# Spectra with exchanged halves, copied by the sync queue, for one full-width cross product in a metaformer block

## The chip, the cores and the metric

The kernel runs on one core of a Trainium2 chip. The metric is the device time of one execution in microseconds (us). A difference of about 0.2% (1.05 us) is what a measurement of this kernel can tell from no change.

The core has five engines that run side by side and wait for each other by semaphores: TensorE (PE, matrix products into PSUM), VectorE (DVE), ScalarE (ACT), GpSimd (POOL) and SyncE (SP), which here only issues transfers. Sixteen DMA engines carry the transfers of all queues.

## The reference, cut to what matters

One block of a network on 16 images of 128 channels and 16x16 pixels: a convolution branch with a Fourier filter, then a mixture of 8 experts with the best two taken for each token.

```python
xp  = star_scale * square(relu(einsum('bhwc,mc->bhwm', xc, w_pw1))) + star_bias   # 256 channels
xf  = rfft2(xp, axes=(1, 2), norm='ortho')
weight         = einsum('bfc,hwf->bhwc', routeing, complex(cw))      # complex, 4 filters mixed
spatial_weight = einsum('bfc,hwf->bhwc', spatial_routeing, spatial_weights)
xs  = irfft2(xf * weight, ...)
out = einsum('bhwm,dm->bhwd', xp * spatial_weight + xs, w_pw2)
x   = x + out
t   = layernorm(tokens(x));  x = x + experts(t)                      # top 2 of 8
```

The part that matters is `xf * weight`, a complex product: `re = xr*wr - xi*wi`, `im = xi*wr + xr*wi`. The second product of each needs the imaginary part where the real part stands, and the other way round.

## The kernel before

**Tiling.** The 16 images are worked on as 8 pairs. In a first stage ("phase A", 0 to about 90 us) each pair's pixels become `star` (the `xp` of the reference) and its spectrum `spec`. For each pair i and each parity e (0 or 1) of the vertical frequency, `spec[:, e, i, :]` is a tile of 128 partitions by 512 columns: the real parts are in partitions 0 to 63 and the imaginary parts in 64 to 127 (a few real-only frequencies fill the rest). Then routing weights are worked out once (90 to 130 us), and each of them is laid out over `RS` by eight small transfers, five on the sync queue and three on GpSimd's (`routing_rows`, line 356).

**The filter stage** ("phase B", 130 to about 217 us) is a software pipeline with one step for each pair (`filter_loop`: steps 0 to 2 written out, 3 to 6 in a loop of two steps, step 7 written out). In step i:

- TensorE makes six weight tiles of pair i+1 (`filters`, L810) in three PSUM banks that are used in turn; n = 0, 1 are the spatial weights, n = 2 and 4 the real parts and n = 3 and 5 the imaginary parts for e = 0 and 1. Between them it projects pair i-1 (L844), turns pair i back to pixels (`branch`, L828 and L834), transposes normalised tokens of pair i-2 (L853) and makes their expert logits (L859).
- VectorE makes the products of pair i+1 for e = 0 (`filter_products`): `prod` = spectrum times real weight (L1095, 128 x 512), and `cross` = exchanged spectrum times imaginary weight, in two instructions of 64 partitions (L1098, L1099), which read one half of the spectrum and write the other half of `cross`. It adds the branch to the tokens of pair i-1 (`residual`, L1104) and takes their statistics (L980, L984), makes the products for e = 1, waits for GpSimd's `rstd` and normalises the tokens of pair i-1 (L990, four instructions of 128 x 128 that write `xn`), and copies logits (L1116).
- GpSimd makes the inverse standard deviation (`inv_std`, L436 and L438), adds `prod` and `cross` of pair i+1 (`spectral`, L499, two instructions) and multiplies `star` with the spatial weights of pair i+2 (`spatial`, L493, two instructions), in this order once a step has its rhythm.
- ScalarE copies between PSUM and SBUF (L620, L625, L630).
- The sync queue stores each pair's normalised tokens (`store_tn`, L399). After the store of pair 5 it issues the loads of the experts' weights `w1` and `w3` (L407, L408), which lie where `star` lay.

**Afterwards** (217 to 257 us) the weights are split into high and low parts and the tokens are sorted by expert; then 71 tiles of tokens run through the experts (257 to 500 us), with indirect gathers and scatters by GpSimd; a last stage adds up the results (to 525 us).

What the steps below touch: `filter_products` and its callers in VectorE's program, `store_tn` and the lines around it in SyncE's, `inv_std`, `spectral` and `spatial` in GpSimd's, `filters` in TensorE's, and the tile `rw2`, a weight that is read for the last time by the matrix products of L785, before `r_mm` is signalled.

## Time and profile before

| what | us |
|---|---|
| median of three runs | 527.25 |
| the three runs | 526.24, 527.25, 527.28 |
| the profiled execution | 526.45 |
| its span in the profile | 524.7 |
| outside the span | 1.75 |

| engine | busy us | share of the span |
|---|---|---|
| PE | 390.1 | 74% |
| DVE | 255.3 | 49% |
| POOL | 246.8 | 47% |
| ACT | 168.1 | 32% |

The shares are means over stages with different limits. The page draws them in 40 slices of 13.1 us; in the slices of the filter stage (130 to 217 us) both PE and DVE show 8 or 9 tenths, and after it DVE falls to 2 or 3. The chain of work that ended last passes in the filter stage mainly through DVE and POOL, and from 257 us on mainly through PE. The clock of PE was granted at full speed (2.4 GHz) from 136.5 to 221.8 us and at half (1.2 GHz) in the 20 us before.

### The profile page before, as it was taken

What the parts mean: (1) busy time and instruction counts of PE and PEld (TensorE: products, weight loads), DVE (VectorE), ACT (ScalarE), POOL (GpSimd) and SP (SyncE); (2) the same over time, 40 slices, a digit from 0 to 9 for tenths busy, and PEclk for the clock granted to TensorE, in tenths of its full rate; (3) what the DMA queues carried; (4) which work ended last, traced back from release to release, by engine and by line L of the source; (5) the groups of instructions that cost most, each with busy time, mean ns of one, the idle gap of its engine ahead of it and who ended that gap; (6) DMA issues with size and microseconds to landing.
All of it is one profiled execution on the core that took longest, in us unless ns stands there. A gap on an engine that the chain in (4) does not pass through costs nothing.

```text
span 524.7 us, 7887 instructions
## 1 busy us (share of the span) xinstructions
PE 390.1 (74%) x2272; PEld 319.2 (61%) x2273; DVE 255.3 (49%) x637; ACT 168.1 (32%) x387; POOL 246.8 (47%) x265
## 2 busy tenths in 40 slices
PE   0899899860999888699497877967878687886700
PEld 0565555650587767556397776867877587875700
DVE  5377664440789999729732322332323332333236
ACT  0544444020123231343043333333323333333233
POOL 7224423412774465100255655556556566664434
PEclk9999999795799999969587979797979988899855
DMA  8910000003001000730011111111111111111184
GB/s 247 223 40 2 0 0 0 6 5 35 2 0 41 20 20 21 280 141 1 15 36 41 47 33 43 35 39 41 35 40 40 40 35 45 40 44 31 36 303 178
DMA packets 14081, 29.94 MB, mean 57 GB/s; under 512 B 4392, under 2 KB 5564, under 8 KB 13548
## 3 DMA queue, kind: packets, MB, share of 16 engines
q1 hardware_dynamic: 7388, 17.93, 11.3%
q0 software_dynamic: 4784, 9.52, 6.7%
q10 hardware_dynamic: 1888, 2.23, 1.2%
q8 instruction: 11, 0.18, 0.1%
q14 instruction: 10, 0.08, 0.0%
HBM read 20.24 MB, written 8.85 MB: 55 GB/s over the span
## 4 chain that ended last, share of the span: by engine, by line
PE 50%; DVE 17%; issue 10%; DMA 6%; another core or an unknown queue 5%; ACT 5%; POOL 4%; SPq 1%; POOLq 1%; DVEq 0%; ACTq 0%
PE bank L953 14%; PE bank L935 11%; DVE xn L990 7%; PE bank L928 6%; PE bank L895 2%; DMA RS<-r_hl 2%; PE bank L783 2%; PE bank L922 2%; PE bank L726 2%; PE bank L734 2%; POOL shared L499 2%; ACT shared L676 2%; DVE st L980 1%; PE bank L914 1%
## 5 line engine op out<-in xcount | busy, mean ns | idle before, releaser
L524 POOL DMA_INDIRECT y_dram<-shared,idx_scatter x71 | 69.9, 985 | 80.0 <-DVE shared L1248 68.2
L935 PE MATMUL bank<-spec,shared 128*128 x426 | 71.6, 311 | 39.0 <-ACT shared L676 36.7
L519 POOL DMA_INDIRECT shared<-tn_dram,idx_gather x71 | 68.8, 969 | 58.8 <-DVE idx_gather L1238 37.4
L935 PEld LDWEIGHTS bank<-spec,shared 128*128 128x128 f32 x426 | 61.3, 216 | 46.1 <-issue 45.7
L1258 DVE TENSOR_TENSOR shared<-shared,bank 128x384 f32<-128x384 f32 x71 | 39.2, 552 | 70.6 <-issue 36.6
L1243 DVE TENSOR_TENSOR xgt_hl<-bank,xgt_hl 128x128 fp32r<-128x128 f32 x71 | 20.7, 291 | 90.2 <-ACT xgt_hl L671 85.1
L953 PE MATMUL bank<-RS,xgt_hl 128*128 x142 | 59.4, 419 | 0.1
L683 ACT ACTIVATE shared<-bank 128x384 f32<-128x384 f32 x71 | 34.8, 491 | 68.3 <-PE bank L953 49.1
L990 DVE TENSOR_SCALAR xn<-T,mv,rstd 128x128 f32<-128x128 f32 (+1 forms) x64 | 51.3, 872 | 3.7 <-POOL rstd L438 3.1
L953 PE MATMUL bank<-w_hi,xgt_hl 128*128 x142 | 51.8, 365 | 0.0
L671 ACT ACTIVATE xgt_hl<-bank 128x128 fp32r<-128x128 f32 x71 | 19.7, 277 | 75.7 <-PE bank L922 57.3
L928 PE MATMUL bank<-ident,shared 128*128 128x128 f32 x213 | 38.1, 291 | 6.9 <-issue 5.1
L676 ACT ACTIVATE shared<-bank 128x384 f32<-128x384 f32 x71 | 35.0, 492 | 22.5 <-PE bank L928 17.0
L953 PE MATMUL bank<-w_lo,xgt_hl 128*128 x142 | 40.0, 366 | 0.0
L810 PE MATMUL bank<-RS,coef 128*128 128x512 f32 (+1 forms) x48 | 21.4, 504 | 22.0 <-DMA RS<-r_hl 15.5
L928 PEld LDWEIGHTS bank<-ident,shared 128*128 128x128 f32 x213 | 29.0, 151 | 13.0 <-issue 8.1
L436 POOL TENSOR_SCALAR var_eps<-mv 128x4 f32<-128x4 f32 x16 | 3.7, 228 | 68.9 <-DVE mv L984 68.8
L745 PE MATMUL bank<-xp,sp 128*64 128x256 f32 x288 | 33.6, 387 | 0.0
L834 PE MATMUL bank<-inv,shared 128*128 128x256 f32 x128 | 30.4, 380 | 1.8 <-POOL shared L499 1.8
L953 PEld LDWEIGHTS bank<-RS,xgt_hl 128*128 128x128 f32 x142 | 30.6, 215 | 1.3 <-issue 1.1
L953 PEld LDWEIGHTS bank<-w_hi,xgt_hl 128*128 128x128 f32 x142 | 30.3, 213 | 0.0
L953 PEld LDWEIGHTS bank<-w_lo,xgt_hl 128*128 128x128 f32 x142 | 28.9, 210 | 0.0
(175 smaller groups left out, 685.2 us busy)
## 6 DMA issues: line engine op xcount, KB each, us to landing
star<-y_dram SPq DMA_DIRECT2D x16, 256.0 KB, 5.5
star<-in_w SPq DMA_DIRECT2D x2, 1536.0 KB, 8.4
tn_dram<-xn SPq DMA_DIRECT2D x8, 256.0 KB, 2.0
out<-T ACTq DMA_DIRECT2D x8, 256.0 KB, 2.5
spec<-in_w SPq DMA_DIRECT2D x1, 1536.0 KB, 7.1
shared<-in_sp_even SPq DMA_DIRECT2D x1, 1280.0 KB, 14.6
shared<-tn_dram,idx_gather POOLq DMA_INDIRECT x71
y_dram<-shared,idx_scatter POOLq DMA_INDIRECT x71
```

Source lines behind the costliest of these rows:

```text
L519: pool.indirect_dma_start(xg[j % BUFS], None, tn_dram, bass.IndirectOffsetOnAxis(ap=idx_gather[:, j:j + 1], axis=0)).then_inc(S[f"g_x{j % ...
L524: pool.indirect_dma_start(y_dram, bass.IndirectOffsetOnAxis(ap=idx_scatter[:, j:j + 1], axis=0), yo[j % BUFS], None).then_inc(S[f"y_out{j ...
L676: act.activation(hidt[u], p_ht[u][:, 0:HID], ACT.Copy).then_inc(S["f_hts"], 1)
L683: act.activation(silu[u], p_h1[u][:, 0:HID], ACT.Silu).then_inc(S["f_silu"], 1)
L745: mm = pe.matmul(ps_conv[u][HALF * g:HALF * g + HALF, 0:PIX], sp1[:, t, :], xp[:, u, g, t // 3:t // 3 + SIZE, t % 3:t % 3 + SIZE], start=( ...
L810: pe.matmul(ps_w[n % 3][:, :], coef[:, ring[n], :], RS[:, :, :, ds(i, 1), :].rearrange("r c g b m -> r g c (b m)"), start=True, stop=True)\
L834: mm = pe.matmul(ps_v[u][m][:, g * PIX:(g + 1) * PIX], y_c[u][e][:, g * MED + m * P:g * MED + (m + 1) * P], inv[:, e, :], start=False, sto ...
L928: mm = pe.transpose(p_ht[u][:, c * P:(c + 1) * P], hid[u][:, c * P:(c + 1) * P], ident[:, :])
L935: mm = pe.matmul(p_y[:, 0:DIM], hidt[u][:, c * P:(c + 1) * P], w2s[:, c, ds(e * DIM, DIM)], start=(c == 0), stop=(c == HC - 1))
L953: mm = pe.matmul(psum[:, 0:HID], xgt[u][xs], w_hl[ws][:, cols], start=(n == 0), stop=(n == 2))
L990: op = dve.tensor_scalar(xn[:, u, t, :], flat(T[:, ds(i * 4 + t, 1), :]), mv[:, u, t, 0:1], rstd[:, u, t:t + 1], ALU.subtract, ALU.mult)
L1258: dve.tensor_tensor(hid[u], silu[u], p_h3[u][:, 0:HID], ALU.mult).then_inc(S["f_act"], 1)
```

## The change

`filter_products` now makes `cross` in one instruction of 128 partitions, from a copy of the spectrum whose halves are exchanged. The copy of pair i, both parities, lies in one of two tiles, `rw2` (even pairs) and a new tile `turned_b` (odd pairs), 4 KiB in each partition. It is made by two transfers of the sync queue, each of 64 partitions x 2 rows x 512 floats (256 KiB), from SBUF to SBUF. The copies of pairs 0 to 3 stand in front of the first token store, that of pair i+4 behind the store of pair i; each waits until the tile's last reader (`b_cross` of pair i-2 of its own number) is through. VectorE waits for the copy by a semaphore for each of the two tiles.

```diff
+        turned_b = sb("turned_b", [P, NF * MED])
+        turned = [t[:].rearrange("p (e n) -> p e n", e=2) for t in (rw2, turned_b)]
...
+            def turn_spectrum(i, u):
+                wait_apart(sp, S["a_spec"], i * 2 + 2)
+                wait_done(sp, S["b_cross"], i * 2 - 2)
+                for lo, hi in ((0, 64), (64, 0)):
+                    sp.dma_start(turned[u][lo:lo + 64], spec[hi:hi + 64, :, ds(i, 1), :].rearrange("p e i n -> p e (i n)"))\
+                        .then_inc(S[f"b_turned{u}"], 16)
...
-            store_tn(0, 0)
-            store_tn(1, 1)
-            with sp.Fori(1, PAIRS // 2 - 1) as n:
-                for u in range(2):
-                    store_tn(n * 2 + u, u)
+            sp.wait_ge(S["r_mm"], 1)
+            for i in range(4):
+                turn_spectrum(i, i % 2)
+
+            def store_and_turn(i, u):
+                store_tn(i, u)
+                if i + 4 < PAIRS:
+                    turn_spectrum(i + 4, u)
+            for i in range(PAIRS - 2):
+                store_and_turn(i, i % 2)
...
-            def filter_products(i, e):
+            def filter_products(i, u, e):
...
                 dve.wait_ge(S["b_w"], i * 6 + n_s + 1)
-                dve.tensor_tensor(cross[e][0:64], spec_at(64, P, e, i), ps_w[n_s % 3][0:64, :], ALU.mult)
-                dve.tensor_tensor(cross[e][64:P], spec_at(0, 64, e, i), ps_w[n_s % 3][64:P, :], ALU.mult)\
+                dve.wait_ge(S[f"b_turned{u}"], (i - u) * 16 + 32)
+                dve.tensor_tensor(cross[e], turned[u][:, e, :], ps_w[n_s % 3][:, :], ALU.mult)\
                     .then_inc(S["b_cross"], 1)
```

How the rows stand on two engines. First VectorE, in the second half of the loop body of the filter stage: the products of e = 0, the residual and its statistics, the products of e = 1. Line numbers of the changed kernel are 18 higher from here on; ISA and REGISTER_ALU rows are register work. Before:

```order
L1095 TENSOR_TENSOR shared<-spec,bank2 128x512
L1097 REGISTER_ALU
L1098 ISA
L1098 TENSOR_TENSOR shared<-spec,bank0 64x512
L1099 TENSOR_TENSOR shared<-spec,bank0 64x512
L1104 ISA
L1104 TENSOR_TENSOR T<-T,bank7 128x512
```

The same place in the changed kernel:

```order
L1113 TENSOR_TENSOR shared<-spec,bank2 128x512
L1115 REGISTER_ALU
L1117 TENSOR_TENSOR shared<-turned_b,bank0 128x512
L1122 ISA
L1122 TENSOR_TENSOR T<-T,bank7 128x512
```

One instruction of 128 partitions stands where two of 64 stood, with one more semaphore in its wait; nothing else of VectorE's order moves. The products of e = 1 change in the same way.

Second SyncE, from the spreading of the routing weights to the experts' weights. Before:

```order
L356 DMA RS<-r_hl 4x32x128 x5
L399 DMA tn_dram<-xn 128x512 x2
...
L399 DMA tn_dram<-xn 128x512
L398 REGISTER_ALU
L399 ISA
L399 DMA tn_dram<-xn 128x512
...
L407 DMA star<-in_w1 128x3072
```

In the changed kernel:

```order
L360 DMA RS<-r_hl 4x32x128 x5
L405 DMA rw2<-spec 64x2x512 x2
L405 DMA turned_b<-spec 64x2x512 x2
L405 DMA rw2<-spec 64x2x512 x2
L405 DMA turned_b<-spec 64x2x512 x2
L410 DMA tn_dram<-xn 128x512
L405 DMA rw2<-spec 64x2x512 x2
L410 DMA tn_dram<-xn 128x512
...
L410 DMA tn_dram<-xn 128x512 x2
L425 DMA star<-in_w1 128x3072
```

Eight pairs of transfers are new; the last of them stands behind the store of pair 3, and between the store of pair 5 and the load of `w1` nothing is new.

## Rows read from the trace of the kernel before

**Rows 1.** Busy time by stretch: us, then PE, PEld, DVE, ACT, POOL, PEclk, DMA share, GB/s.

```profile
144.90:157.10 12.20, 11.97 (x75) 10.56 (x76) 10.40 (x19) 3.06 (x6) 8.73 (x8) 1.00 0.00 0
189.75:200.76 11.01, 9.61 (x60) 8.13 (x59) 10.62 (x20) 2.90 (x5) 6.19 (x6) 1.00 0.06 24
```

**Rows 2.** DVE in order of time, one step: start us, us, line, operation [idle before].

```profile
189.86 0.68 DVE L1095 TENSOR_TENSOR shared<-spec,bank 128x512 f32<-128x512 f32 x1
190.57 0.68 DVE L1098 TENSOR_TENSOR shared<-spec,bank 64x512 f32<-64x512 f32 x1
191.26 0.69 DVE L1099 TENSOR_TENSOR shared<-spec,bank 64x512 f32<-64x512 f32 x1
191.99 0.69 DVE L1104 TENSOR_TENSOR T<-T,bank 128x512 f32 x1
...
193.76 0.38 DVE L984 BATCH_NORM_AGGREGATE mv<-st 128x2 f32<-128x6 f32 x4
194.13 0.69 DVE L1095 TENSOR_TENSOR shared<-spec,bank 128x512 f32<-128x512 f32 x1
194.85 0.68 DVE L1098 TENSOR_TENSOR shared<-spec,bank 64x512 f32<-64x512 f32 x1
195.54 0.69 DVE L1099 TENSOR_TENSOR shared<-spec,bank 64x512 f32<-64x512 f32 x1
196.27 4.46 DVE L990 TENSOR_SCALAR xn<-T,mv,rstd 128x128 f32 x4
```

**Rows 3.** POOL in order of time, the same step.

```profile
194.29 0.23 POOL L436 TENSOR_SCALAR var_eps<-mv 128x4 f32<-128x4 f32 x1 [4.66 <-DVE mv L984]
194.68 1.04 POOL L438 TENSOR_TENSOR rstd<-var_eps,mhalf 128x4 f32<-128x4 f32 x1 [0.15 <-POOL var_eps L436]
195.69 2.49 POOL L499 TENSOR_TENSOR shared<-shared 128x512 f32<-128x512 f32 x2
198.15 2.49 POOL L493 TENSOR_TENSOR shared<-star,shared 128x512 f32<-128x512 f32 x2
```

**Rows 4.** L990 where POOL is idle (215 to 217 us): duration ns min/median/max.

```profile
L990 DVE TENSOR_SCALAR xn<-T,mv,rstd x4: 337/340/347, 215.7 to 216.5; 128x128 f32<-128x128 f32 x4
```

**Rows 5.** Phase A, DVE and POOL at 61 us: the race behind rstd.

```profile
61.20 1.56 DVE L990 TENSOR_SCALAR xn<-T,mv,rstd 128x128 f32 x2
61.35 1.33 POOL L444 TENSOR_TENSOR buf<-star 128x512 f32 x1 [0.25 <-DVE star L997]
```

**Rows 6.** The second half of cross, all 16: duration ns, first and last start us.

```profile
L1099 DVE TENSOR_TENSOR shared<-spec,bank x16: 691/692/692, 133.2 to 206.5; 64x512 f32<-64x512 f32 x16
```

**Rows 7.** PE in order of time: the transposed tokens, then the two waits of a step.

```profile
190.05 0.60 PE L853 MATMUL bank<-ident,xn 128*128 128x128 f32 x4
...
194.87 0.50 PE L810 MATMUL bank<-RS,coef 128*128 x1 [0.48 <-DVE shared L1095]
196.29 0.51 PE L810 MATMUL bank<-RS,coef 128*128 x1 [0.92 <-DVE shared L1099]
```

**Rows 8.** PE in order of time at the start of the filter stage.

```profile
130.12 3.19 PE L810 MATMUL bank<-RS,coef 128*128 128x512 f32 x6 [15.46 <-DMA RS<-r_hl]
133.11 3.54 PE L734 MATMUL bank<-buf,fwd 128*128 128x512 f32 x4
137.44 0.97 PE L810 MATMUL bank<-RS,coef 128*128 128x512 f32 x3 [0.78 <-DVE spec L1003]
```

**Rows 9.** DVE in order of time there: cross of pair 0, spectrum of pair 7.

```profile
132.50 0.68 DVE L1098 TENSOR_TENSOR shared<-spec,bank 64x512 f32<-64x512 f32 x1
...
136.05 1.33 DVE L1003 COPY spec<-bank 128x512 f32<-128x512 f32 x2
```

**Rows 10.** DVE in order of time: cross of pair 2, behind PE.

```profile
147.19 0.68 DVE L1098 TENSOR_TENSOR shared<-spec,bank 64x512 f32<-64x512 f32 x1 [1.59 <-PE bank L810]
```

**Rows 11.** Busy time by stretch: loads of 128 and 64 partitions, the wait for RS.

```profile
8.00:11.00 3.00, 0.00 (x0) 0.00 (x0) 3.00 (x6) 0.00 (x0) 3.00 (x2) 1.00 1.07 398
17.00:22.00 5.00, 5.00 (x27) 2.99 (x27) 1.82 (x4) 2.23 (x4) 0.74 (x1) 1.00 0.97 203
122.00:130.00 8.00, 0.00 (x0) 0.00 (x0) 0.00 (x0) 0.00 (x0) 0.00 (x0) 0.50 0.24 26
```

**Rows 12.** SP's queue in order of time: w1 is issued.

```profile
210.49 0.35 SPq L407 DMA_DIRECT2D star<-in_w  x1
```

**Rows 13.** ACT in order of time: the first use of w1.

```profile
217.11 2.76 ACT L648 ACTIVATE RS<-star 128x3072 fp32r<-128x3072 f32 x1 [2.89 <-DMA star<-in_w]
```

More of the change, by code:

```diff
@@ L333, in metaformer @@
             "r_log r_max r_sub r_exp r_sum r_rec r_norm r_tr r_hi r_lo r_rows r_rows_pool b_w b_sw b_p b_cross b_u b_y "
-            "b_vt b_vts b_w2 b_t b_stats b_aggr b_eps b_rstd b_norm b_tn0 b_tn1 b_tr b_tnt "
+            "b_vt b_vts b_w2 b_t b_stats b_aggr b_eps b_rstd b_norm b_turned0 b_turned1 b_tn0 b_tn1 b_tr b_tnt "
             "b_gate b_logit q_iota q_zero q_tri q_dve q_ready q_exp_done q_count q_oh_tile q_oh_ready q_oh_used "
@@ L1154, in phase_b @@
                 if not last(i, PAIRS):
-                    filter_products(i + 1, 0)
+                    filter_products(i + 1, 1 - u, 0)
                 if not first(i):
@@ L1158, in phase_b @@
                 if not last(i, PAIRS):
-                    filter_products(i + 1, 1)
+                    filter_products(i + 1, 1 - u, 1)
                 else:
@@ L1168, in phase_b @@
                     logit_copy(i - 2, u)
-            filter_products(0, 0)
-            filter_products(0, 1)
+            filter_products(0, 0, 0)
+            filter_products(0, 0, 1)
             spectrum_copy(PAIRS - 1)
```

## The prediction

> **What bounds the kernel now.** I read the page first (shares by engine, the 40 slices, the chain that ended last), then the busy time by stretch, then one step of the filter stage in order of time on DVE, POOL and PE. The page says that no engine bounds the whole; the stretches say where this change can act. In a steady step of the filter stage, 11.01 us long, DVE is busy 10.62 us, PE 9.61 and POOL 6.19 [rows 1]. But DVE's busy time is not all work. The four instructions of L990 take 4.46 us in it [rows 2], and 0.34 us each where POOL is idle [rows 4]. In the step they end one by one at the ends of POOL's four instructions of L499 and L493, which run back to back from 195.69 to 200.64 us [rows 3]: each L990 waits until the POOL instruction that was running before it has ended. So the step is a ring of two engines:
>
> DVE makes prod and cross of e = 0 and the residual (189.86 to 192.68), statistics (to 194.14) [rows 2]; POOL makes rstd (to 195.72), then L499 twice and L493 twice (to 200.64) [rows 3]; the last L990 ends with them at 200.73, and DVE begins the next step.
>
> Two things follow. The cross of e = 0 lies on this ring. The cross of e = 1 (194.85 to 196.23) does not: it lies beside POOL's rstd and the first L499, and what it gives back is waited away again in front of L990.
>
> The filter stage is followed by a chain that begins with its end: the store of pair 5's tokens, the issue of w1 at 210.49, w1's first use at 217.11 [rows 12, 13].
>
> **The change part by part.**
>
> *The cross of e = 0.* From the start of L1098 to the start of the residual are 191.99 - 190.57 = 1.42 us [rows 2]. One instruction of 128 x 512 from SBUF and PSUM, as L1095 is, takes 0.68 to 0.69 us, and with the gap behind it 0.71 (190.57 - 189.86) [rows 2]. So a step loses 1.42 - 0.71 = 0.71 us. The ring's other parts keep their lengths: behind the statistics come 0.15 us, L436, L438 and the 4.95 us of L499 and L493 as before.
>
> How many steps get it? The products of eight pairs are made, 16 second halves in all [rows 6]. For pairs 0 and 1 PE is the bound (below). For pair 2 the cross starts at 147.19, behind PE's weight tile [rows 10], and PE has no gap in the whole of that step (11.97 of 12.20 us [rows 1]); but the residual stands behind the cross on DVE and needs only PE's projection, which has ended by then, so this cross already shortens the ring. Pairs 2 to 7 make six steps: 6 x 0.71 = 4.26 us.
>
> *The cross of e = 1.* It would end at 195.54 instead of 196.23, and the norm behind it needs rstd, which ends at 195.72 [rows 2, 3]. DVE then meets POOL's first L499, which started at 195.69, and waits for its end as it does now. Gain nothing. What hides it: POOL's 1.04 us of L438. The two numbers are close, which makes the first rival below.
>
> *PE.* Its slack decides how much of the ring's gain is kept. In a step PE waits 0.48 us for prod of e = 1 and 0.92 us for cross of e = 1 [rows 7]. In the new step of 10.30 us its waits move: it gets to the second weight tile later against the ring and waits for less there, and the transposes of xn, at 190.05 just behind the end of the norm at 189.7 [rows 7], wait for it. Its work is 9.61 us [rows 1] in 10.30, so 0.7 us stay. PE is next in line but not the bound. In the first steps it is: the forward transform of pair 7 (L734) runs from 133.11 to 136.65, and then the copy of its spectrum, 1.33 us for two, releases the next weight tiles at 137.44 [rows 8, 9]. With both crosses of pair 0 shorter by 0.7 us, DVE would reach that copy at 134.65 instead of 136.05, but the second half of the copy needs PE's 136.65, so it ends at 137.35 against 137.38. Gain nothing. It also leaves room: the first cross can start 1.2 us late and nothing moves.
>
> *The transfers.* Each pair's copy is 512 KiB in two transfers of 64 partitions. The trace has no transfer between partitions of this shape; the nearest are the loads into 64 partitions at 17 to 22 us, at 203 GB/s, against 398 GB/s of loads into 128 [rows 11]. At 203 GB/s a pair takes 2.6 us, at 398 GB/s 1.3 us. I take the slow one, since the shape is its shape. From pair 2 on it is hidden: copy 2 is issued when cross of pair 0 is done (about 135 us) and needed at 147.19 [rows 10]; copy i+4 is issued behind the store of pair i, at the end of step i+1, and needed in step i+3, with a whole step of 10.3 us between. On SP's queue the stores stay in front of their copies, and no copy stands in front of w1. If that cover were gone, a step would lose the rest of 2.6 us and a fixed latency.
>
> Pairs 0 and 1 are the exposed ones. They are issued right behind the RS transfers, which end at 130.1 and for which PE waits 15.46 us [rows 8]. Copy 0 is needed at 132.50 [rows 9]. If it only starts when RS is through, it ends at 130.0 + 2.6 = 132.6 plus some tenths, which the 1.2 us of room take up. What it may do to RS itself lies between nothing (the DMA engines are 24% busy at 26 GB/s while PE waits, so there is room beside [rows 11]) and 1 MiB at 203 GB/s = 5.2 us, if all four transfers went in front. They stand behind on the same queue, so I take 0.2 us.
>
> A rule that speaks against the change: rows 11 show half the rate for half the partitions. By the Trainium skill, "SBUF — State Buffer", section "Door 1: The DMA port swizzle", 64 partitions reach 8 of the 16 ports, about 200 GB/s at 1 MiB, and by its section "Can I just issue two DMAs to hit both halves?" two such transfers serialize; the trace agrees with the first (203 GB/s), and two loads of 64 partitions each, one for either half, were under way there. With the fixed 2 us of a transfer that the same page of the Trainium skill gives (section "The DMA setup-cost knee"), an estimate, copy 0 would end near 134.6 and the stage would lose 0.9 us; no row here shows that for a queue that is already running.
>
> *The end of the stage.* The norm of pair 5 ends six shortened steps after pair 2's cross, 4.26 us earlier, and with it w1, whose transfer is the next link [rows 12, 13]. All behind it moves as a block. PE's clock may fall at slightly other points of the expert tiles; I give that plus or minus 1 us and no sign.
>
> *Sum.* -4.26 + 0.2 = -4.1 us. The profiled execution (span 524.7 and 1.75 outside) took 526.45 and would take 522.4. The four executions known have a mean of 526.8; against the median of 527.25 the profiled one is 0.8 low, and I put the new median at 522.7.
>
> **The rivals.**
>
> *A: the norm gets in before POOL.* If DVE's first L990 starts before POOL's first L499, it takes 0.34 us and only three wait, so the norm ends one POOL instruction (1.25 us) earlier. For it: in phase A, where DVE waits for rstd too, L990 started at 61.20 and POOL's L444 at 61.35; two L990 took 1.56 us, so the first was free and the second was held [rows 5]. Against it: there POOL had its wait for star behind rstd; here L499 starts at 195.69, even before L438's row ends at 195.72 [rows 3], and DVE needs a semaphore first. That the first to start keeps the other out is also what the Trainium skill says of the pair of ports that DVE and GpSimd share ("SBUF — State Buffer", "Who interferes with whom"). Then PE is the bound at some 9.6 us [rows 1], 0.7 less than 10.3, in five steps: 522.7 - 3.5 = 519.2.
>
> *B: the copies start late or slowly.* Transfers between partitions may run slower than loads, say at 100 GB/s (between 26 and 203 [rows 11]): copy 0 takes 5.2 us, ends at 135.2, 2.7 us late, less 1.2 of room = 1.5 us; or RS is pushed back by a part of the 5.2 us. 522.7 + 1.8 = 524.5, up to 525.4.
>
> *C: slower than before.* The four copies share the DMA engines with the RS transfers, three of which run on POOL's queue, and RS ends later by their whole 5.2 us; PE, DVE and POOL all wait for that. It decides against the change from 4.3 us on. 522.7 + 5.2 = 527.9. For it: nothing else is on the path there. Against it: queue order, and DMA engines that are 76% idle [rows 11].
>
> *D: the change doesn't give what it says.* A ring that I haven't seen (PE through the transposes and logits, or ScalarE's copies) holds 11 us, and the 0.7 us come back as a wait: 526.8.
>
> **How the numbers follow.** Forecast 0.70 (522.7, its own range 521.4 to 524.0), A 0.08, B 0.12, C 0.06, D 0.04. The forecast and B are 0.82, so the range is 520.6 to 525.4, from the forecast with 1 us of clock and one of execution below it, to B's upper end. About 0.2% (1.05 us) is what a measurement of this kernel can tell from no change. Faster by more: forecast, A and B = 0.90. Within: D = 0.04. Slower by more: C = 0.06, of which a part lies within, left as it is.
>
> **What would show each step.** The steady step is 10.3 us instead of 11.0; the cross is one row of 0.69 us; DVE waits 0.1 to 0.2 us for rstd in front of L990 (now it never does), and four L990 still take 4.8 to 4.9 us from rstd's end to the norm's. The second weight tiles at 137.44 start at the same time. RS releases PE at 130.1 to 130.5. A first step of 9.6 us would show A; a DVE wait for a DMA at 132.5, B; a wait of PE for RS beyond 16 us, C; steps of 11 us, D. I am wrong in the main point if the cross of e = 0 turns out not to be on the ring, that is if rstd starts 0.7 us earlier and the norm doesn't end earlier.

## The result, and the profile after

The changed kernel takes 520.66 us (median of eleven runs, 518.24 to 524.63), the kernel before on the same chip 526.26 us (eleven runs, 522.2 to 528.48): a ratio of 0.987, 95% interval 0.9844 to 0.9896 (the two medians by themselves give 0.989). On the median of 527.25 us that stood ahead of the prediction this is 520.4 us, just under the lower end of the range (520.6), and the interval reaches from 519.0 to 521.8. The forecast was 0.9% faster and it became 1.3%: the sign was right, and so was the place of the gain; its size was not, and a loss in another place had been put near nothing. The profiled execution took 520.77 us, with a span of 519.0 against 524.7 us.

The page of the changed kernel, its parts 1, 3, 4 and 6 in extract (part 6: KB each, median us from issue to landing):

```profile
span 519.0 us, 7883 instructions
PE 378.6 (73%) x2272; PEld 309.1 (60%) x2273; DVE 244.7 (47%) x621; ACT 167.7 (32%) x387; POOL 246.6 (48%) x265
q1 hardware_dynamic: 9692, 22.13, 15.6%
PE 52%; DVE 13%; issue 11%; DMA 7%; another core or an unknown queue 6%; ACT 5%; POOL 3%; SPq 1%; ACTq 0%; DVEq 0%; POOLq 0%
rw<-spec SPq DMA_DIRECT2D x8, 256.0 KB, 3.8
turned_b<-spec SPq DMA_DIRECT2D x8, 256.0 KB, 3.8
```

DVE is busy 10.6 us less than before. Sixteen instructions of 0.69 us are gone [rows 6]: 11.0 us. The sixteen transfers of 256 KB are the copies; in the median one has landed 3.8 us after its issue.

One steady step of the filter stage, busy time by stretch and then DVE, POOL and PE in order of time; these answer to rows 1, 2, 3 and 7:

```profile
188.74:198.67 9.93, 9.45 (x58) 7.96 (x58) 9.31 (x19) 2.88 (x6) 6.19 (x6) 1.00 0.28 79
```

```profile
188.64 0.18 DVE L1134 COPY logits<-bank 128x32 f32 x1
188.74 0.67 DVE L1113 TENSOR_TENSOR shared<-spec,bank 128x512 f32<-128x512 f32 x1
189.33 0.68 DVE L1117 TENSOR_TENSOR shared<-rw,bank 128x512 f32<-128x512 f32 x1
189.93 0.68 DVE L1122 TENSOR_TENSOR T<-T,bank 128x512 f32 x1
...
192.66 0.68 DVE L1117 TENSOR_TENSOR shared<-rw,bank 128x512 f32<-128x512 f32 x1
193.76 4.89 DVE L1008 TENSOR_SCALAR xn<-T,mv,rstd 128x128 f32 x4 [0.42 <-POOL rstd L456]
198.57 0.18 DVE L1134 COPY logits<-bank 128x32 f32 x1
198.67 0.67 DVE L1113 TENSOR_TENSOR shared<-spec,bank 128x512 f32<-128x512 f32 x1
```

```profile
192.61 1.04 POOL L456 TENSOR_TENSOR rstd<-var_eps,mhalf 128x4 f32<-128x4 f32 x1 [0.15 <-POOL var_eps L454]
193.62 2.50 POOL L517 TENSOR_TENSOR shared<-shared 128x512 f32<-128x512 f32 x2
196.08 2.49 POOL L511 TENSOR_TENSOR shared<-star,shared 128x512 f32<-128x512 f32 x2
```

```profile
188.85 0.65 PE L871 MATMUL bank<-ident,xn 128*128 128x128 f32 x4 [0.47 <-DVE xn L1008]
```

The step has 9.93 us where it had 11.01 [rows 1], and 10.3 were forecast. The cross (L1117) is one instruction. DVE now waits 0.42 us for rstd, then the four instructions of the norm (L1008, before L990) end with POOL's four, as in [rows 2, 3]. What was not forecast stands in the starts: from prod to cross 0.59 us, and to the residual (L1122) 0.60, where [rows 2] have 0.71 and 0.72 around the halves.

The start of the filter stage, SP's queue, PE, and busy time by stretch (the stretch of before follows in a fence of its own; PE answers to rows 8):

```profile
115.15 2.99 SPq L360 DMA_DIRECT2D RS<-r_hl  x5
118.24 1.45 SPq L405 DMA_DIRECT2D rw<-spec  x2
119.74 3.84 SPq L405 DMA_DIRECT2D turned_b<-spec  x2
```

```profile
133.67 3.19 PE L828 MATMUL bank<-RS,coef 128*128 128x512 f32 x6 [19.63 <-DMA RS<-r_hl]
136.66 2.96 PE L752 MATMUL bank<-buf,fwd 128*128 128x512 f32 x4
140.41 0.97 PE L828 MATMUL bank<-RS,coef 128*128 128x512 f32 x3 [0.78 <-DVE spec L1021]
```

```profile
118.00:132.00 14.00, 0.00 (x0) 0.00 (x0) 0.00 (x0) 0.00 (x0) 2.60 (x3) 0.51 0.89 89
```

```profile
118.00:130.00 12.00, 0.00 (x0) 0.00 (x0) 0.00 (x0) 0.00 (x0) 3.22 (x4) 0.50 0.35 39
```

PE waits 19.63 us for RS instead of 15.46 [rows 8]. While it waits, the DMA engines are busy 89% of the time, in the kernel before 35%. So the change lost at this place and gained more than forecast in the steps. The stages side by side, from the traces of both kernels:

| stage, us | before | after | difference |
|---|---|---|---|
| first issue of RS to PE's first filter matmul | 14.36 | 18.52 | +4.16 |
| from there to the end of pair 5's norm | 79.65 | 72.97 | -6.68 |
| from there to the first expert tile | 50.55 | 48.27 | -2.28 |
| the expert tiles | 228.4 | 227.8 | -0.7 |

Pair 5's norm ends at 206.64 instead of 209.77 us: 3.1 us earlier, of the 5.7 us that the span lost (the first issue of RS alone comes 0.6 us earlier in this trace).

### The profile page after: what moved, and what is told of

Its sections match the earlier page's. It is cut to its first block, busy times and chain, and to the rows that moved or that the text cites. A ratio compares the mean times of both kernels' runs of the same rounds, so it can differ in the third digit from the quotient of the medians.

```text
span 519.0 us, 7883 instructions
## 1 busy us (share of the span) xinstructions
PE 378.6 (73%) x2272; PEld 309.1 (60%) x2273; DVE 244.7 (47%) x621; ACT 167.7 (32%) x387; POOL 246.6 (48%) x265
## 4 chain that ended last, share of the span: by engine, by line
PE 52%; DVE 13%; issue 11%; DMA 7%; another core or an unknown queue 6%; ACT 5%; POOL 3%; SPq 1%; ACTq 0%; DVEq 0%; POOLq 0%
PE bank L971 12%; PE bank L953 9%; DVE xn L1008 6%; PE bank L946 4%; PE bank L852 3%; DMA RS<-r_hl 3%; PE bank L752 3%; PE bank L940 2%; PE bank L801 2%; PE bank L828 2%; PE bank L744 2%; PE bank L913 2%; PE bank L877 2%; DMA star<-in_w 1%
## 5 line engine op out<-in xcount | busy, mean ns | idle before, releaser
L953 PE MATMUL bank<-spec,shared 128*128 x426 | 68.0, 300 | 36.5 <-ACT shared L694 26.3
L953 PEld LDWEIGHTS bank<-spec,shared 128*128 128x128 f32 x426 | 57.9, 206 | 44.5 <-issue 44.3
L971 PE MATMUL bank<-RS,xgt_hl 128*128 x142 | 57.7, 406 | 0.3
L1008 DVE TENSOR_SCALAR xn<-T,mv,rstd 128x128 f32<-128x128 f32 (+1 forms) x64 | 54.1, 916 | 5.8 <-POOL rstd L456 5.5
L971 PE MATMUL bank<-w_hi,xgt_hl 128*128 x142 | 50.5, 355 | 0.0
L946 PE MATMUL bank<-ident,shared 128*128 128x128 f32 x213 | 37.2, 285 | 14.9 <-DVE shared L1276 13.7
L828 PE MATMUL bank<-RS,coef 128*128 128x512 f32 (+1 forms) x48 | 19.5, 489 | 20.6 <-DMA RS<-r_hl 19.6
L971 PEld LDWEIGHTS bank<-RS,xgt_hl 128*128 128x128 f32 x142 | 29.2, 206 | 1.8 <-issue 1.4
L971 PEld LDWEIGHTS bank<-w_hi,xgt_hl 128*128 128x128 f32 x142 | 29.2, 205 | 0.0
L511 POOL TENSOR_TENSOR shared<-star,shared 128x512 f32<-128x512 f32 x16 | 20.0, 1274 | 17.3 <-ACT shared L638 17.3
```

The source lines that it names most:

```text
L828: pe.matmul(ps_w[n % 3][:, :], coef[:, ring[n], :], RS[:, :, :, ds(i, 1), :].rearrange("r c g b m -> r g c (b m)"), start=True, stop=True)\
L946: mm = pe.transpose(p_ht[u][:, c * P:(c + 1) * P], hid[u][:, c * P:(c + 1) * P], ident[:, :])
L953: mm = pe.matmul(p_y[:, 0:DIM], hidt[u][:, c * P:(c + 1) * P], w2s[:, c, ds(e * DIM, DIM)], start=(c == 0), stop=(c == HC - 1))
L971: mm = pe.matmul(psum[:, 0:HID], xgt[u][xs], w_hl[ws][:, cols], start=(n == 0), stop=(n == 2))
L1008: op = dve.tensor_scalar(xn[:, u, t, :], flat(T[:, ds(i * 4 + t, 1), :]), mv[:, u, t, 0:1], rstd[:, u, t:t + 1], ALU.subtract, ALU.mult)
```

## The experiments

Each kernel ran beside the kernel before on its chip, and not all on the same chip. Three things were in question: what the copies cost beside the RS transfers, why a step lost 1.07 us and not 0.71, and whether four POOL instructions really hold the norm. The stages of all kernels, from one trace of each (in us; the "step" is a steady one):

| kernel | RS issue to PE | PE to norm of pair 5 | step | norm to first expert tile |
|---|---|---|---|---|
| before | 14.36 | 79.65 | 11.01 | 50.55 |
| after | 18.52 | 72.97 | 9.94 | 48.27 |
| copies first | 14.45 | 73.51 | 9.94 | 50.54 |
| copies unused | 18.45 | 79.60 | 11.00 | 50.22 |
| no copies | 14.45 | 73.50 | 9.94 | 50.12 |
| two halves | 18.95 | 78.84 | 10.89 | 47.50 |
| halves swapped | 14.40 | 78.90 | 10.89 | 51.28 |
| copies after RS | 14.72 | 75.41 | 9.94 | 46.33 |
| one copy beside RS | 17.51 | 72.01 | 9.95 | 51.71 |
| sum early | 14.50 | 66.51 | 8.83 | 46.08 |
| after, again | 18.46 | 73.27 | 9.95 | 49.18 |
| copies first, again | 14.64 | 73.24 | 9.94 | 50.29 |
| before, again | 14.59 | 79.63 | 11.00 | 50.77 |

**Copies first.** The copies of pairs 0 and 1 stand in front of the RS transfers in SP's program.

```diff
+            sp.wait_ge(S["r_mm"], 1)
+            turn_spectrum(0, 0)
+            turn_spectrum(1, 1)
             routing_rows(sp, range(5), "r_rows")
...
-            sp.wait_ge(S["r_mm"], 1)
-            for i in range(4):
+            for i in range(2, 4):
                 turn_spectrum(i, i % 2)
```

> The changed kernel, but the copies of pairs 0 and 1 stand in front of the five RS transfers on the sync queue instead of behind them (they can go as soon as r_mm is signalled, some 5 us before RS can be issued). Theory S (the copies behind RS share the DMA engines with it and make it late): in the changed kernel PE started its first weight tile 18.5 us after the first RS issue, before the change 14.4; here it is 14.4 to 15.5 again, steps stay 9.93 us, and the time is 3 to 4 us under the changed kernel, some 9 to 10 us (1.8%) under the kernel before. Theory N (RS is late by chance or by the allocation of the new tile, not by the copies): still 18.5 and the time of the changed kernel.

Measured: 514.22 us (median of six) against 523.12 of before, ratio 0.9816 (0.9774 to 0.9858). PE, in order of time:

```profile
129.86 3.19 PE L829 MATMUL bank<-RS,coef 128*128 128x512 f32 x6 [15.55 <-DMA RS<-r_hl]
```

The wait for RS is back at its old length, and the steps keep the new one. That rules out the new tile and chance as reasons for the late RS.

**Copies unused.** The copies run as in the change, but DVE makes its two halves from the spectrum, as before.

```diff
                 dve.wait_ge(S[f"b_turned{u}"], (i - u) * 16 + 32)
-                dve.tensor_tensor(cross[e], turned[u][:, e, :], ps_w[n_s % 3][:, :], ALU.mult)\
+                dve.tensor_tensor(cross[e][0:64], spec_at(64, P, e, i), ps_w[n_s % 3][0:64, :], ALU.mult)
+                dve.tensor_tensor(cross[e][64:P], spec_at(0, 64, e, i), ps_w[n_s % 3][64:P, :], ALU.mult)\
```

> The changed kernel with all its copies and waits, but VectorE makes cross in two instructions of 64 partitions from the spectrum itself, as before the change; the copies are not read. Theory S: RS releases PE 18.5 us after its first issue, steps are 11.0 us, and the time is 4.2 us (0.8%) over the kernel before. Rival (the copies cost nothing, the whole change of the time is VectorE's): the time of the kernel before. If the last stages had become faster by the copies, the time would be under it by 2 to 3 us.

Measured: 526.17 us, ratio 1.0061 (1.003 to 1.0092), so 0.6% slower than before. PE, in order of time:

```profile
133.63 3.19 PE L828 MATMUL bank<-RS,coef 128*128 128x512 f32 x6 [19.55 <-DMA RS<-r_hl]
```

The price of the copies stands alone here: 4.1 us in front of PE (18.45 against 14.36), nothing behind it (79.60 against 79.65). The time rose by 3.1 us by the medians, where 4.2 were expected; the interval (1.6 to 4.8 us) covers both.

**No copies.** No transfer, and DVE multiplies the spectrum of the same partitions. The exchange of the halves is left out of the computation.

```diff
-            for i in range(4):
-                turn_spectrum(i, i % 2)
...
-                if i + 4 < PAIRS:
-                    turn_spectrum(i + 4, u)
...
-                dve.wait_ge(S[f"b_turned{u}"], (i - u) * 16 + 32)
-                dve.tensor_tensor(cross[e], turned[u][:, e, :], ps_w[n_s % 3][:, :], ALU.mult)\
+                dve.tensor_tensor(cross[e], spec_at(0, P, e, i), ps_w[n_s % 3][:, :], ALU.mult)\
```

> The changed kernel without any copy: cross is one instruction of 128 partitions that reads the spectrum without the exchange, so that part of the computation is left out. Theory S: RS releases PE after 14.4 us; steps 9.93 us; the time is 6.5 us under the kernel before by the six shorter steps, and 4.2 us under the changed kernel. If the step were shortened by the copy's place and not by the width and the aligned partitions, it would be 11.0.

Measured: 515.27 us, ratio 0.9829 (0.9793 to 0.9865). With the copies first and with none at all the two stages agree to 0.01 us (14.45, then 73.51 and 73.50). Copies in that place cost nothing, and from pair 2 on nothing anywhere. The kernel without copies also lacks the wait for them in front of the cross, so that wait has no part in the length of the step.

**Two halves.** The copies run and are used, but the cross is two instructions of 64 partitions, both operands on the same partitions.

```diff
-                dve.tensor_tensor(cross[e], turned[u][:, e, :], ps_w[n_s % 3][:, :], ALU.mult)\
+                dve.tensor_tensor(cross[e][0:64], turned[u][0:64, e, :], ps_w[n_s % 3][0:64, :], ALU.mult)
+                dve.tensor_tensor(cross[e][64:P], turned[u][64:P, e, :], ps_w[n_s % 3][64:P, :], ALU.mult)\
```

> The changed kernel, but cross is again made in two instructions of 64 partitions, which read the copy at the partitions that they write. Theory H (an instruction that begins at another partition than the last one that read or wrote that memory starts only when everything before it has ended, about 0.1 us later): prod to first half 0.60 us start to start (not held), first to second half 0.70, second half to residual 0.72, last L990 to the logits' copy 1.33; step 9.93 + 0.7 + 0.3 = 10.9 us. Rival X (it is reading one half of the partitions and writing the other that costs the 0.1 us): all start-to-start distances 0.60, the last one 1.22, step 10.5 us.

Measured: 522.37 us in one run. DVE, in order of time:

```profile
192.96 0.68 DVE L1113 TENSOR_TENSOR shared<-spec,bank 128x512 f32<-128x512 f32 x1
193.55 0.67 DVE L1117 TENSOR_TENSOR shared<-rw,bank 64x512 f32<-64x512 f32 x1
194.24 0.69 DVE L1118 TENSOR_TENSOR shared<-rw,bank 64x512 f32<-64x512 f32 x1
194.96 0.69 DVE L1123 TENSOR_TENSOR T<-T,bank 128x512 f32 x1
...
199.11 4.58 DVE L1008 TENSOR_SCALAR xn<-T,mv,rstd 128x128 f32 x4
203.72 0.19 DVE L1135 COPY logits<-bank 128x32 f32 x1
```

The first half starts 0.59 us after prod, as in the changed kernel; the second half starts 0.69 us after it, and the residual 0.72 us after that, as in the kernel before. What this one early start is worth shows in the step: 10.89 instead of 11.01.

**Halves swapped.** The kernel before, with nothing changed but the order of its two half instructions.

```diff
-                dve.tensor_tensor(cross[e][0:64], spec_at(64, P, e, i), ps_w[n_s % 3][0:64, :], ALU.mult)
-                dve.tensor_tensor(cross[e][64:P], spec_at(0, 64, e, i), ps_w[n_s % 3][64:P, :], ALU.mult)\
+                dve.tensor_tensor(cross[e][64:P], spec_at(0, 64, e, i), ps_w[n_s % 3][64:P, :], ALU.mult)
+                dve.tensor_tensor(cross[e][0:64], spec_at(64, P, e, i), ps_w[n_s % 3][0:64, :], ALU.mult)\
```

> The kernel before the change with one edit: of the two instructions of cross the one that writes partitions 64 to 127 comes first. The same work, the same number of instructions. Theory H (an instruction is held until all before it have ended if its first partition differs from that of the last instruction that read or wrote the same memory): the last product now reads PSUM from partition 0, so the logits' copy behind the norm is no longer held: last L990 to that copy 1.22 us instead of 1.33, and the steady step is 10.90 instead of 11.01. The time falls by 0.5 to 0.7 us, less than can be measured. Rival X (any exchange between halves costs its 0.1 us, whatever the order): 1.33 and 11.01 as before.

Measured: 523.43 us against 521.95, ratio 1.0017 (0.9981 to 1.0054): no difference that can be told. But the trace has it. DVE, in order of time:

```profile
194.91 4.46 DVE L990 TENSOR_SCALAR xn<-T,mv,rstd 128x128 f32 x4
199.30 0.18 DVE L1116 COPY logits<-bank 128x32 f32 x1
```

From the last L990's start to the copy of the logits (L1116) are 1.22 us; in the kernel before 1.34. The copy begins before the norm's modelled end in the one (199.30 against 199.37) and behind it in the other. The step is 10.89 us. Between these two instructions nothing was edited; what differs at the copy is which half of PSUM DVE had read last (its last operands in SBUF are those of the norm, the same in both).

**Copies after RS.** The first four copies wait until all RS transfers have landed.

```diff
             sp.wait_ge(S["r_mm"], 1)
+            sp.wait_ge(S["r_rows"], 16 * 5)
+            sp.wait_ge(S["r_rows_pool"], 16 * 3)
             for i in range(4):
```

> The changed kernel, but SyncE waits until all eight RS transfers have landed before it issues the copies of pairs 0 and 1. Theory S: RS releases PE 14.4 us after its first issue. The room of 1.2 us in front of the first cross is then tested: a pair's copy takes 3.8 us from issue to landing in the changed kernel's later steps, and its second transfer is issued 0.6 us later, so cross of pair 0 starts at about 4.5 us behind PE's start instead of 2.3, and the norm of pair 5 ends about 1 us later against PE's start than with the copies in front (73.5 us). If RS were late for another reason, 18.5 us stay.

Measured: 511.12 us in one run. DVE, in order of time:

```profile
130.49 0.69 DVE L1115 TENSOR_TENSOR shared<-spec,bank 128x512 f32<-128x512 f32 x1 [15.44 <-PE bank L830]
133.56 0.69 DVE L1119 TENSOR_TENSOR shared<-rw,bank 128x512 f32<-128x512 f32 x1 [2.38 <-DMA rw<-spec]
```

RS is undisturbed (14.72 us), and now the copy itself is on the path: DVE waits 2.38 us for it. The norm of pair 5 ends 1.9 us later against PE's start than with the copies first (75.41 against 73.51), where about 1 us was expected. Not all of that is the copy's. The first step, from the first prod of a pair to that of the next, is 0.6 us longer (7.19 against 6.62) and the second 1.3 us (7.80 against 6.47); in the second no transfer is waited for, and PE's granted clock is at half from 137.7 to 141.1 us, where it is at full speed with the copies first. Whether the late copy brought that fall is not shown. The profiled execution is 5.2 us shorter than that of copies first, on another chip: 4.2 us of it lie in the stretch behind the stage (46.33 us), of which more below, 2.2 in the expert tiles and 1.3 in front of RS.

**One copy beside RS.** Only the copy of pair 0, half the bytes, stands right behind RS; the others wait until RS has landed.

```diff
-            for i in range(4):
+            turn_spectrum(0, 0)
+            sp.wait_ge(S["r_rows"], 16 * 5)
+            sp.wait_ge(S["r_rows_pool"], 16 * 3)
+            for i in range(1, 4):
```

> The changed kernel, but only the copy of pair 0 (512 KiB) stands right behind RS; that of pair 1 waits until RS has landed. Theory S with a cost by bytes: half of the 4.1 us, so RS releases PE about 16.4 us after its first issue. If the cost came from the number of transfers or from those at the end of the queue alone, it would be 14.4 to 15; if any copy beside RS costs all of it, 18.5.

Measured: 520.77 us in one run; RS to PE 17.51 us. Half the bytes cost 3.1 us and all of them 4.1, where a cost by bytes had let 16.4 us be expected, so the delay does not go by the bytes alone.

**Sum early.** Copies first, and POOL adds prod and cross of e = 0 in front of rstd instead of behind it.

```diff
-            def spectral(i, u):
-                for e in range(2):
+            def spectral(i, u, parities):
+                for e in parities:
...
                     spatial(i + 1, 1 - u)
+                if not last(i, PAIRS):
+                    spectral(i + 1, 1 - u, (0,))
                 if not first(i):
                     inv_std("b_aggr", "b_eps", "b_rstd", LN_T_EPS, i - 1, 1 - u)
                 if not last(i, PAIRS):
-                    spectral(i + 1, 1 - u)
+                    spectral(i + 1, 1 - u, (1,))
             spatial(0, 0)
-            spectral(0, 0)
+            spectral(0, 0, range(2))
```

> The kernel with the copies in front of RS, and GpSimd adds prod and cross of e = 0 in front of the standard deviation, where it idles 4.7 us in a step, instead of behind it. Theory R (the ring: behind rstd stand four GpSimd instructions, and each holds one instruction of the norm): with three behind rstd the fourth norm instruction takes 0.34 us and runs free, the norm ends about 0.95 us earlier in a step, unless PE becomes the bound: step 9.0 to 9.6 us instead of 9.94, 5 steps, 2 to 4.5 us less than with the copies in front alone (ratio to before 0.973 to 0.978). If the norm were bound by something else, the step stays at 9.94.

Measured: 505.75 us (median of six, 503.13 to 506.95) against 521.95, ratio 0.967 (0.9624 to 0.9716). POOL, DVE in order of time, and the step by stretch:

```profile
175.61 1.04 POOL L457 TENSOR_TENSOR rstd<-var_eps,mhalf 128x4 f32<-128x4 f32 x1 [0.15 <-POOL var_eps L455]
176.62 1.26 POOL L518 TENSOR_TENSOR shared<-shared 128x512 f32<-128x512 f32 x1
179.62 2.50 POOL L512 TENSOR_TENSOR shared<-star,shared 128x512 f32<-128x512 f32 x2 [1.74 <-ACT shared L641]
```

```profile
176.78 1.95 DVE L1011 TENSOR_SCALAR xn<-T,mv,rstd 128x128 f32 x4 [0.44 <-POOL rstd L457]
...
179.34 0.69 DVE L1116 TENSOR_TENSOR shared<-spec,bank 128x512 f32<-128x512 f32 x1 [0.51 <-PE bank L831]
181.25 0.69 DVE L1120 TENSOR_TENSOR shared<-rw,bank 128x512 f32<-128x512 f32 x1 [1.22 <-PE bank L831]
```

```profile
172.00:180.83 8.83, 8.83 (x60) 8.04 (x59) 6.55 (x18) 2.79 (x5) 6.23 (x7) 1.00 0.34 94
```

Only one POOL instruction stands right behind rstd (the next wait 1.74 us for ACT), and the norm takes 1.95 us instead of 4.89: its first instruction is still held, the other three take 0.34 us each. DVE now waits for PE, and PE has no gap in the step. The step is 8.83 us. That is more than was expected (9.0 to 9.6 us, ratio 0.973 to 0.978): three POOL instructions were to stand behind rstd, and the wait for ACT left one.

**Once more, on another chip.** The changed kernel, copies first and the kernel before, none of them edited further.

> The changed kernel once more, beside the next two on one chip. From the end of pair 5's norm to the first expert tile it took 48.3 us in its profile, the kernel before 50.6, and this gap of 2.3 us is what the shorter steps and the late RS don't explain. Theory C (chance of PE's clock: the stretch at half clock there was 3.4 us long in the one profile and 10.2 in the other, and it depends on when in its own rhythm the chip lowers the clock, not on the kernel): profiles of any of the kernels show now one length and now the other; the ratio to before is 0.990 to 0.995 if the means are even, since the steps and RS leave 2.5 us. Rival (the change shortens this stretch each time): 48.3 us again, ratio 0.987.

> The kernel with the copies in front of RS once more. By its stretches it should be 4.1 us (0.8%) faster than the changed kernel on the same chip; the two ratios to before, taken on different chips, gave 0.6%. Theory S with nothing else: ratio 0.980 to 0.983 and 0.8% under the changed kernel. If the changed kernel has another gain that this one lacks: 0.4% or less under it.

> The kernel before once more, for a second profile. RS 14.4 us, steps 11.01. Theory C: the stretch from the norm of pair 5 to the first expert tile lies anywhere from 46 to 52 us, with the length of the half-clock stretch behind it (0, 3.4, 10.2 or 13.7 us). Rival: 50.6 us again.

Measured, against 472.65 us of before: the change 468.89, ratio 0.989 (0.9853 to 0.9927); copies first 464.48, ratio 0.983 (0.9803 to 0.9857); before again 471.72 in one run. The ratios agree with those of the first chips within their intervals (the medians by themselves give 0.992 and 0.983), and copies first gains another 4.4 us by the medians. Everything up to the expert tiles is as long as before; the expert tiles take 174.1 to 174.5 us instead of 223 to 228.

## Why the prediction was right in its place and wrong in its size

**The ring: right.** The prediction said that a step is a ring of DVE and POOL, and that the norm cannot end before POOL's four instructions. Against copies first, sum early changed nothing but where one of them stands, and the norm fell from 4.89 to 1.95 us. The small gap was foreseen too: DVE waits for rstd, 0.42 us where 0.1 to 0.2 were said, since two late starts of the kind told of below went on the way to the cross of e = 1 as well.

**The cross of e = 1: right.** It ends at 193.34 us, rstd at 193.65, and what it gives back is waited away. Rival A came close and did not happen: POOL's L517 starts at 193.62 us, DVE's first L1008 at 193.76.

**"So a step loses 1.42 - 0.71 = 0.71 us": wrong.** This is the term that was mis-sized; a step lost 1.07 us. The prediction took the instruction that goes away and left the starts of its neighbours as they were. From prod's start to the residual's, the kernel before has 191.99 - 189.86 = 2.13 us [rows 2], the changed one 189.93 - 188.74 = 1.19 us: 0.94 us less. The remaining 0.12 us lie between the norm and the copy of the logits, which is on the ring too: 1.34 us from the last norm's start before, 1.22 after. A full-width DVE instruction starts 0.59 or 0.60 us after the last one when nothing holds it, although it takes 0.68. The two half instructions each start on other partitions than the one before them, and so does the instruction behind them; these starts come 0.69 to 0.72 us apart, behind the end of the one before. Call such a late start a held one. Two halves gives back one of the three held starts, halves swapped another one, and each makes the step 10.89 instead of 11.01: a held start costs 0.11 to 0.12 us here, and three of them are the missing 0.36. The Trainium skill, "VectorE: DVE Perf Modes", section "Two Vector instructions with no wait between them", has this rule: an instruction is held until all earlier ones of VectorE have finished if its operands in a memory start in another quadrant of partitions than those last read or written there. The traces agree in each of the starts named, also in the one of the logits' copy, which is held by the last PSUM operand that the second half had read. The prediction had read 0.71 as the length of an instruction "with the gap behind it"; it was the length with a hold. The distances that decide were measured; the rule is what foretold which of them would move, and halves swapped bore it out.

**Six steps: right.** From the prod of pair 2 on, the five steps of the changed kernel are shorter by 0.93, 1.05, 1.06, 1.06 and 1.07 us, and the rest up to pair 5's norm by 0.94: 6.1 us where 4.26 were said. Copies first loses 6.14 us from PE's start to pair 5's norm. Pairs 0 and 1 gave nothing there, as said: its first two steps have 6.62 and 6.47 us, before 6.67 and 6.46. In the changed kernel the first one has 6.09. That is a gift of PE's clock: the forward transform in front of the second weight tiles takes 2.96 us instead of 3.54 [rows 8], with a granted clock of 0.76 from 137.40 to 140.41 us, where the kernel before had 0.64 from 134.00 to 137.44.

**"I take 0.2 us" for the copies beside RS: wrong by 3.9 us.** This is the second mis-sized term, with the other sign. The mechanism is that of rival C, at 4.1 us just under the 4.3 from which it would have decided. The prediction rested on the queue's order and on idle DMA engines. By the trace's semaphore events each RS transfer of SP's queue ends with 4 counts, one for each DMA engine that carries it, and each copy with 16. So the copies ran on twelve engines that had no RS transfer of SP's queue in front of them, beside RS and not behind it, and the busy share rose to 0.89. The time from the issue of an RS transfer to its landing, in the kernel before and in the changed one; it is known only for the three on GpSimd's queue:

```profile
DMA to landing us min/median/max: 5.1/6.4/10.7
```

```profile
DMA to landing us min/median/max: 5.2/7.3/14.3
```

The longest of the three takes 3.6 us more. Of the five on SP's queue the last count comes at 133.58 us instead of 130.03, and PE starts 0.09 us behind it in both kernels: these are the ones that PE waits for. The share of 0.24 in the prediction's own stretch [rows 11] was a mean over engines of which some had all the work: it is that of 3.8 of 16 engines, and 3.5 of these are packets of SP's RS transfers, which have four. The Trainium skill has this too ("DMA: Bandwidth & Descriptors", section "Why a DMA increments its semaphore by 16 and not by 1"): a transfer uses the largest number of engines up to 16 that divides the slowest dimension of both its sides; for four partitions that is four, and the trace agrees.

The queue's order itself held on RS's four engines. Of the 32 counts of pair 0's copy 24 come by 127.80 us and 8 between 133.60 and 135.21, just behind RS's last: as many as two transfers have on four engines. Pair 1's copy has 24 and 8 as well. What became longer are RS's own packets, 640 of 512 bytes in SP's transfers: 0.068 us each in the mean before, 0.098 in the changed kernel, 0.091 with one copy and 0.070 with the copies first. Over four engines that is 4.8, 3.6 and 0.3 us more for each (an estimate), near the 4.1, 3.1 and 0.1 us that RS came later. So RS did not stand behind the copies; each of its packets was slower while other engines copied. What the packets share, and why half the bytes cost three quarters of the delay, stays open.

**The copies themselves: too cheap, but hidden.** 2.6 us for a pair were said; a transfer takes 3.8 us from issue to landing, its fixed part included. Where one was exposed (copies after RS), DVE waited 2.38 us for it. In the change it is never waited for, but by little: pair 0's copy has its last count at 135.21 us, and its cross starts at 135.95. The prediction's B also has a slip: 1.5 us late became 1.8 in its sum.

**"All behind it moves as a block": not so.** The sum of the errors at pair 5's norm is small: -6.68 + 4.16 = -2.5 us between the two stages against the forecast's -4.1. On that alone the profiled execution would have taken 523.9 us. Most of the rest came from behind it, 2.3 us of it before the expert tiles, where the prediction allowed plus or minus 1 us for all that follows. Busy time by stretch from 206 us on in the changed kernel, and from 209 us on in the kernel before:

```profile
206.00:226.00 20.00, 13.30 (x75) 10.98 (x76) 11.56 (x49) 8.35 (x8) 2.59 (x5) 0.91 0.70 256
```

```profile
209.00:229.00 20.00, 13.53 (x73) 11.48 (x74) 11.09 (x46) 8.48 (x8) 2.73 (x5) 0.82 0.75 273
```

The work is the same and the granted clock is not. About where PE waits for ACT's copies behind the norm and then makes the gates, its clock falls to half, from 217.3 to 220.8 us in the changed kernel and from 221.8 to 232.0 in the kernel before. Over all traces this stretch is 46.1 to 46.3 us long with no such fall (copies after RS, sum early), 47.5 to 48.3 with one of 3.4 us (after, two halves), 49.2 with 6.8 (after, again), 50.1 to 50.8 with 10.2 (before twice, copies first twice, copies unused, no copies) and 51.3 to 51.7 with 13.7 (halves swapped, one copy). So the stretch goes with the length of the fall, by more than 5 us in all, nearly as much as the whole change. Whether the change itself shortens it stays open. The changed kernel had 3.4 us in one trace and 6.8 in another, the kernel before 10.2 in both; copies first, which reaches this place with the same steps as the changed kernel, had 10.2 twice. The runs on the second chip were to decide it and did not: if the clock fell by chance the ratio was to be 0.990 to 0.995, if the change shortens the fall it was to be 0.987 with 48.3 us once more, and 0.989 and 49.2 us were measured. The kernel before gave 50.8 us, the value named for a fall that belongs to the kernel. Two traces of a kernel don't settle that. They do show why the ratio of the change (0.987) need not be that of its two stages (-2.5 us, 0.995). Copies first has the same fall of the clock as the kernel before in both its traces, is 6.1 us shorter in the two stages (73.51 + 14.45 against 79.65 + 14.36), and its ratios of 0.982 and 0.983 stand for 8 to 10 us. On the second chip, where both have a trace, its span is 7.4 us shorter, and the stages place nearly all of it: 0.7 us in front of RS's first issue, 6.3 in the two stages, 0.5 from there to the expert tiles. The medians there differ by 8.2 us. On the first chips no trace of the kernel before stands beside it, and what its ratio shows above the stages is not placed.

**So the range was missed** by two terms of the sum that were wrong in opposite directions (-1.9 us over six steps, up to 0.36 in each, and +3.9 us once), which together would have made the time higher than forecast, and by a stretch behind the stage that was taken to move as a block. That the time came so near the range is luck: the errors of the two terms cancel in part, and most of the rest goes with a shorter fall of PE's clock, which nothing in the prediction has.

## What to carry to other kernels

When an instruction of VectorE goes away, read the distances between the starts around it and not its length: two half-partition instructions each start late, and so does the one behind them. A mean busy share of the DMA engines can hide that four of sixteen have all the work. A queue's order did not protect a small transfer on four engines from a large one on sixteen, although it held on the four; a load for which an engine waits wants nothing wide issued right behind it, and here the same copies were free in front of it. Where one engine's instructions are held by those of another, it can pay to move the other engine's work away from that place: with the copies first, one POOL instruction in front of rstd instead of behind it took another 7.0 us off the stage (73.51 to 66.51), where the one-instruction cross had taken 6.1, and the ratio went from 0.982 to 0.967.

## What the runs showed of the hardware that was not expected

- A full-width DVE instruction of 0.68 us can start 0.59 us after the one before it; a held one starts 0.69 to 0.72 us after it. The order of two half instructions decides about a copy that stands several instructions behind them (1.22 or 1.34 us).
- Four transfers of 256 KB issued behind eight of 64 KB delay the last of these by 4.1 us; two by 3.1. On the engines that both use the order of the queue holds, and yet the small packets take 0.098 us instead of 0.068. In the changed kernel one of the copies' issues took SP 2.37 us instead of the usual 0.61:

```profile
L405 SPq DMA_DIRECT2D turned_b<-spec x8: 590/610/2372, 119.7 to 189.8; - x8
```

- The chips differ by 10% in this kernel (471.7 to 472.7 us against 522 to 526), all of it in the expert tiles. The costliest group of the page, POOL's scatter, in the changed kernel on the first chip and then on the other (idle time before it, and what ended most of it):

```profile
L542 POOL DMA_INDIRECT y_dram<-shared,idx_scatter x71 | 69.9, 985 | 79.3 <-DVE shared L1266 63.9
```

```profile
L542 POOL DMA_INDIRECT y_dram<-shared,idx_scatter x71 | 70.1, 987 | 26.3 <-DVE shared L1266 17.2
```

  The instruction takes the same time on both; what is waited for in front of it does not. Which part of the chip makes the difference is not known from these runs. The ratios of the kernels agree on both within their intervals.
